# L1 attention on one core: each score bank gets the sums of q from TensorE, not from a VectorE copy

## What is computed

```python
q, vf, vb = (v[:, :, :h], v[:, :, h:2 * h], v[:, :, 2 * h:])
k = x[:, :, None, :] * wk[None, None]
a = -sum_w |q[b,s,h,w] - k[b,t,h,w]| / sqrt(64)      # for all s, t
a = concatenate([a, zeros((b, 1, t, h))], axis=1)
a = softmax(a, axis=1)[:, :t]
bf = einsum('bsdh,bshw->bdhw', a, vf)
bb = einsum('bdsh,bshw->bdhw', a, vb)
```

## Time and profile before

| what | value |
|---|---|
| median of 3 runs | 8382.76 us (8380.82 to 8383.2) |
| the profiled execution's own time | 8385.55 us |
| its span in the trace | 8383.8 us |
| mean granted TensorE clock | 0.989 |
| PE busy | 8146.3 us, 97% of the span |
| PEld busy (beside PE) | 3446.9 us, 41% |
| DVE busy | 7988.7 us, 95% |
| ACT busy | 7685.1 us, 92% |
| POOL busy | 39.7 us |

### The profile page before, as it was taken

How to read it: one execution, slowest core, us unless ns; L and a number is a source line. 1 busy time by engine, 2 the same in 40 slices (tenths; PEclk the granted TensorE clock), 3 DMA queues, 4 the chain that set the end, 5 groups by cost and what they waited for, 6 DMA issues and landing times. The chain is left out here.

```text
span 8383.8 us, 244371 instructions
## 1 busy us (share of the span) xinstructions
PE 8146.3 (97%) x108456; PEld 3446.9 (41%) x108456; DVE 7988.7 (95%) x6906; ACT 7685.1 (92%) x3712; POOL 39.7 (0%) x36
## 2 busy tenths in 40 slices
PE   8699999999999999999999999999999999999999
PEld 3244444444444444444444444444444444444443
DVE  4699999999999999999999999999999999999984
ACT  3599999999999999999999999999999999999986
POOL 1000000000000000000000000000000000000000
PEclk9899999999999999999999999999999999999999
DMA  4310101001010100101010010101001010100000
GB/s 130 102 25 2 25 2 25 2 2 25 2 25 2 25 2 2 25 2 25 2 25 2 2 25 2 25 2 25 2 3 24 2 25 2 25 2 2 2 20 8
DMA packets 150392, 142.53 MB, mean 17 GB/s; under 512 B 115384, under 2 KB 121528, under 8 KB 148776
## 3 DMA queue, kind: packets, MB, share of 16 engines
q1 hardware_dynamic: 135711, 105.19, 5.4%
q10 hardware_dynamic: 13584, 21.06, 0.9%
HBM read 84.15 MB, written 42.05 MB: 15 GB/s over the span
## 5 line engine op out<-in xcount | busy, mean ns | idle before, releaser
L919 ACT ACTIVATE ring<-qx,xs 128x3000 f32<-128x3000 f32 x2624 | 7168.6, 2789 | 358.1 <-PE sc L867 357.5
L867 PE MATMUL sc<-ring,window 128*32 128x375 f32 x90112 | 7329.8, 479 | 118.9 <-DVE ring L956 114.8
L1013 DVE TENSOR_SCALAR ring<-qx,xs 128x3000 f32<-128x3000 f32 x2624 | 4711.7, 1832 | 1.5 <-PE sc L867 1.3
L867 PEld LDWEIGHTS sc<-ring,window 128*32 128x32 f32 x90112 | 2895.8, 109 | 4278.9 <-issue 3709.6
L956 DVE SCALAR_TENSOR_TENSOR ring<-qx,xs,ring 128x3000 f32<-128x3000 f32 x384 | 1284.1, 3344 | 13.5
L953 DVE TENSOR_SCALAR ring<-qx,xs,ratio 128x750 f32<-128x750 f32 x1536 | 925.5, 668 | 21.1 <-issue 15.7
L943 DVE TENSOR_SCALAR sc<-kept,kx 128x750 f32<-128x750 f32 x385 | 385.8, 1002 | 0.6
L985 DVE STREAM_TRANSPOSE exts<-ex 128x768 f32<-128x768 f32 x385 | 374.5, 973 | 0.6
L829 PEld LDWEIGHTS acc<-exts,vf 128*32 128x32 f32 x12480 | 283.0, 109 | 119.9 <-issue 118.7
L815 PE MATMUL acc<-ex,vb 128*32 128x376 f32 x3088 | 314.3, 478 | 1.5 <-DVE ex L972 1.5
L829 PE MATMUL acc<-exts,vf 128*32 128x96 f32 (+1 forms) x12480 | 310.6, 244 | 0.2 <-DVE exts L985 0.2
(11 more groups left out here) (170 smaller groups left out, 915.8 us busy)
## 6 DMA issues: line engine op xcount, KB each, us to landing
qx<-scratch_qk SPq DMA_DIRECT2D x240, 187.5 KB
scratch_v<-exts SPq DMA_DIRECT2D x17, 960.0 KB, 7.8
scratch_qk<-qx ACTq DMA_DIRECT2D x32, 375.0 KB, 6.3
vb<-scratch_v SPq DMA_DIRECT2D x240, 46.0 KB
vf<-scratch_v SPq DMA_DIRECT2D x120, 88.0 KB
scratch_v<-qx SPq DMA_DIRECT2D x4, 960.0 KB, 6.6
scratch_v<-qx ACTq DMA_DIRECT2D x4, 960.0 KB, 8.9
qx<-scratch_qk ACTq DMA_DIRECT2D x16, 187.5 KB
```

The source lines that it names most:

```text
L867: mm = pe.matmul(bank[32 * j:32 * j + 32, h, 0:HALF], window[:, min(part, 1), HALF_NH * g + j, QUADS - 1 - quad:QUADS + 31 - quad], ring[: ...
L919: act.activation(flat(ring[:, k % RING, :, :]), flat(qx[g][:, part, :, :]), ACT.Abs, bias=xs[g][:, 1, part, c:c + 1], scale=0.5).then_inc( ...
L1013: vec.tensor_scalar(flat(ring[:, k % RING, :, :]), flat(qx[g][:, part, :, :]), xs[g][:, 0, part, c:c + 1], xs[g][:, 1, part, c:c + 1], ALU ...
```

## The change

The sums of q no longer go through `kept` and VectorE. After its first step in each tile, TensorE adds them to the score bank itself: eight bf16 products of `select` with `ksum`. `ksum` now holds the 24 rows of the pair with `g` = 0 in partitions 0 to 63 and those of the pair with `g` = 1 in 64 to 127, so that both are there at the same time, and each product reads 64 rows. Step 0 of a tile begins the bank anew (`start=True`). The key terms leave the bank: they are now the per-partition bias of the exponential. `fill` and the semaphore `bank_set` are gone; TensorE waits at a tile's start for the exponential of the tile that used this bank before (`ex_made`). `invert` moves from step 9 to step 8, right behind `add_one`. In the pair's last tile, `add_one` now stands ahead of `key_sums`.

```diff
         if part == 0:
-            queue.dma_start(self.ksum[0:6 * HALF_NH, :], scratch_ks[...
+            queue.dma_start(self.ksum[64 * g:64 * g + 6 * HALF_NH, :], scratch_ks[6 * HALF_NH * g:6 * HALF_NH * (g + 1),
...
-        EXP_AT, FILL_AT, Z_AT, RZ_AT, A_AT, EXT_AT, KEEP_AT = 6, 8, 8, 9, 10, 12, 14
+        EXP_AT, FILL_AT, Z_AT, RZ_AT, A_AT, EXT_AT, KEEP_AT = 6, 8, 8, 8, 10, 12, 14
...
                 def sums(g, b):
                     pe.wait_ge(pair_in[g], b * (16 * NLOADS) + 16 * NLOADS)
-                    for h in range(2):
-                        for j in range(HALF_NH):
-                            mm = pe.matmul(kept[32 * j:32 * j + 32, h, 0:HALF], select[:, 32 * j:32 * j + 32],
-                                           ksum[:, h * HALF:(h + 1) * HALF], start=True, stop=True)
...
-                    pe.wait_ge(bank_set, T + 1)
+                    pe.wait_ge(ex_made, T + 1)
                     if t == NT - 1:
-                        pe.wait_ge(bank_set, (n + 1) * NT)
+                        pe.wait_ge(kx_made, n + 2)
                         sums(1 - g, b + g)
...
-                                               start=False, stop=(i == rows(t) - 1), skip_group_check=True)
+                                               start=(i == 0), stop=(i == rows(t) - 1), skip_group_check=True)
                         mm.then_inc(ring_free, 1 if t < NT - 1 or i < rows(t) - 1 else 1 + TURN - STEPS)
+                        if i == 0:
+                            for h in range(2):
+                                for j in range(HALF_NH):
+                                    pe.matmul(bank[32 * j:32 * j + 32, h, 0:HALF], select[64 * g:64 * g + 64, 32 * j:32 * j + 32],
+                                              ksum[64 * g:64 * g + 64, h * HALF:(h + 1) * HALF],
+                                              start=False, stop=False, skip_group_check=True)
...
-                                   ACT.Exp, scale=-2.0 / D ** 0.5,
+                                   ACT.Exp, scale=-2.0 / D ** 0.5, bias=kx[:, g, t:t + 1],
...
-                    vec.tensor_scalar(kx[:, g, :], kept[:, 0, KX:KX + NT], -0.5, None, ALU.mult).then_inc(kx_made, 1)
-
-                def fill(pairs, g, t):
-
-                    par = t % 2
-                    vec.wait_ge(kx_made, pairs)
-                    if merged(t):
-                        vec.tensor_scalar(sc[par][:, :, 0:HALF], kept[:, :, 0:HALF], kx[:, g, t:t + 1], None,
-                                          ALU.add).then_inc(bank_set, 1)
...
+                    vec.tensor_scalar(kx[:, g, :], kept[:, 0:NT], 1.0 / D ** 0.5, None, ALU.mult).then_inc(kx_made, 1)
...
-                            if due(FILL_AT, i, t):
-                                vec.wait_ge(ex_made, n * NT + (t + 2))
-                                if t == NT - 1:
-                                    key_sums(n + 2, 1 - g)
-                                    fill(n + 2, 1 - g, 0)
-                                else:
-                                    fill(n + 1, g, t + 1)
                             if due(Z_AT, i, t):
                                 add_one(T, par)
+                            if due(FILL_AT, i, t) and t == NT - 1:
+                                vec.wait_ge(ex_made, n * NT + (t + 2))
+                                key_sums(n + 2, 1 - g)
```

More of the change, by code:

```diff
@@ L126, in load_part @@
         if part == 0:
-            queue.dma_start(self.ksum[0:6 * HALF_NH, :], scratch_ks[6 * HALF_NH * g:6 * HALF_NH * (g + 1),
+            queue.dma_start(self.ksum[64 * g:64 * g + 6 * HALF_NH, :], scratch_ks[6 * HALF_NH * g:6 * HALF_NH * (g + 1),
                                                                     bass.ds(b * L, L)]).then_inc(into, 16)
@@ L734, in phase_attend @@
         acc = [psum(ctx, f"acc{k}", [128, 512]) for k in range(2)]
-        kept = psum(ctx, "kept", [128, 2, 512])
+        kept = psum(ctx, "kept", [128, 512])
         turn_c = semaphore(ctx, "turn_c")
@@ L781, in _ @@
                 sp.sem_inc(group_done, NG)
-                sp.sem_inc(ex_made, 1)
                 sp.sem_inc(a_made, 1)
@@ L838, in sums @@
                     pe.wait_ge(pair_in[g], b * (16 * NLOADS) + 16 * NLOADS)
-                    for h in range(2):
-                        for j in range(HALF_NH):
-                            mm = pe.matmul(kept[32 * j:32 * j + 32, h, 0:HALF], select[:, 32 * j:32 * j + 32],
-                                           ksum[:, h * HALF:(h + 1) * HALF], start=True, stop=True)
                     for j in range(HALF_NH):
                         for part in range(2):
-                            mm = pe.matmul(kept[32 * j:32 * j + 32, 0, KX:KX + NT],
+                            mm = pe.matmul(kept[32 * j:32 * j + 32, 0:NT],
                                            window[:, part, HALF_NH * g + j, QUADS - 1:QUADS + 31],
@@ L898, in _, with finish @@
             def _(act):
-                def finish(par, done):
+                def finish(g, t, done):
+                    par = t % 2
                     act.wait_ge(ring_free, done)
                     act.activation(ex[par][:, :].rearrange("p (h c) -> p h c", h=2)[:, :, 0:HALF], sc[par][:, :, 0:HALF],
-                                   ACT.Exp, scale=-2.0 / D ** 0.5,
+                                   ACT.Exp, scale=-2.0 / D ** 0.5, bias=kx[:, g, t:t + 1],
                                    accum_out=zsum[:, par:par + 1]).then_inc(ex_made, 1)
@@ L921, in pair @@
                             if due(EXP_AT, i, t):
-                                finish((t + 1) % 2, n * TURN + (first_step(t) + RING))
+                                if t == 0:
+                                    act.wait_ge(kx_made, n + 2)
+                                if t:
+                                    finish(g, t - 1, n * TURN + (first_step(t) + RING))
+                                else:
+                                    finish(1 - g, NT - 1, n * TURN + RING)
+                act.sem_inc(ex_made, 1)
                 with act.Fori(0, B) as b:
@@ L927, in _ @@
                 act.wait_ge(ring_free, NPAIR * TURN + RING)
-                finish((NT - 1) % 2, NPAIR * TURN + RING)
+                finish(1, NT - 1, NPAIR * TURN + RING)
             @block.vector
@@ L1035, in pair @@
                                 keep(n, 1 - g, b + g)
+                vec.memset(kx[:, 1, :], 0.0).then_inc(kx_made, 1)
                 key_sums(1, 0)
-                fill(1, 0, 0)
                 with vec.Fori(0, B) as b:
@@ L1547, in arrange @@
             if not on_scalar(p % QUADS, part):
-                lo = 3 * (HALF_NH * part + p // 32)
-                select[lo:lo + 3, p] = -0.5
+                for pair in range(2):
+                    lo = 64 * pair + 3 * (HALF_NH * part + p // 32)
+                    select[lo:lo + 3, p] = -0.5
     avg, fant, pick = np.zeros((128, 128), f), np.zeros((128, 128), f), np.zeros((128, NE, 128), f)
```

3 lines of the change are left out of this document (removed).

## The result

The changed kernel takes **8468.4 us** (median of 4 runs, 8466.2 to 8474.7) against 8383.0 us, a ratio of **1.0102** (95% interval 1.0089 to 1.0114): 85 us slower. The forecast was 8493 us.

A forecast was written before the change was run, and what follows sets the result against it. VectorE was taken to bound the kernel, with TensorE 97.7% full. 479.3 + 24 x 0.65 = 494.9 us a pair against 488.0, 110 us in all, gave 8382.8 + 110 = 8493 us, range 8428 to 8548 us.

The forecast's parts named there:

- The bound, and the room: VectorE sets the pace at 20.52 us a tile; TensorE's own work is 476.9 of 488.0 us a pair.
- The 0.46 us that were subtracted from each gap: In TensorE's weight-load waits for VectorE's merged step, 0.46 us of each gap was taken as no loss.
- the 11.1 us: TensorE's lost time a pair before the change, the larger part claimed at the pairs' ends, 4.5 us on average there.
- VectorE's saving: Removed copy saves 0.91 us a tile, 0.13 us come back; VectorE's tile 19.74 us, 0.78 us less, turning into waits.
- The addition A: Time the eight products add to TensorE per tile: 0.32 us of slots plus 0.33 us of size changes, 0.65 us.
- Two changes around the eight products make 0.32 us: Going from 128 to 64 array rows and back loses 0.16 us each time; 0.33 us was taken.
- the mean of five losses in the other layers: Gaps of 0.19, 0.10, 0.14, 0.21 and 0.15 us between differently sized groups in first and last layers, mean 0.16 us.
- the forecast's sum: A pair takes 476.9 - 0.32 + 2.7 = 479.3 us plus 24 tiles' additions: 494.9 us, against 488.0.
- The ends of the pairs: VectorE stays late there; TensorE's losses fall from 3.3 and 5.7 us to 1.4 and 3.9, 2.7 us on average.
- The signs that were named: Profile after: VectorE waits hundreds of us, merged-step waits a few, 0.45 to 0.5 us after products, pair 494 to 496 us.
- costlier rival: Eight products add 0.85 us a tile, or the ring's turn is too tight: +187 us, some 8565 us; chance 0.1.
- The exponential: ScalarE's exponential gets a bias operand at no cost, covered by 298.5 us of ScalarE waiting in 6500.

The follow-up runs named there:

- the last experiment: Changed kernel, but VectorE copies in 19 tiles of a pair and 128-row products run only in tiles 0, 1, 7, 13 and 19: 8321.0 us.

## Why the prediction was right

- **The bound, and the room.** Right: TensorE's room was 488.0 - 481.1 = 6.9 us a pair, less than the 24 additions take. The 0.46 us that were subtracted from each gap had given 20.52 - 0.14 = 20.38 us for the most common tile; the run without the products shows 20.42. One reading was wrong: "the larger part of the 11.1 us" is not at the ends of the pairs. By the forecast's own numbers 4.5 us are there. The gaps ahead of tiles 7, 13 and 19, behind the tiles without a `forward`, are 1.87, 1.41 and 1.42 us before (medians), which is 3.3 us of loss a pair. This is the room that the last experiment uses.
- **VectorE's saving.** Right in size and in worth: the copy is gone, the waits moved to VectorE, and putting the work back cost 32 us.
- **The addition A, 0.65 us a tile.** The mechanism was right and the size off: 0.55 us in a full tile. The slots measured 0.32 as taken; the two changes measured 0.23, not 0.33. The step that mis-sized it is "Two changes around the eight products make 0.32 us": the mean of five losses in the other layers, whose weights have 64 or 128 columns. The same rows show why those were dearer. About 0.10 us pass ahead of a group's first product at each change (31.72 - 31.30 = 0.42 us for a slot of 0.32), whatever the columns. The group's first slot is longer besides, and that grows with the columns: by 0.10 us with 128 (31.30 - 30.88 = 0.42), by 0.05 with 64 (32.09 - 31.72 = 0.37), by 0.02 with 32, as seen above. Together that is 0.20, 0.15 and 0.12 us a change, close to the 0.18, 0.13 and 0.11 us that one such load stands with.

```profile
30.88 0.60 PE L283 MATMUL ps<-x,w1b 10*128 10x375 f32 x4
31.30 0.49 PE L283 MATMUL ps<-x,w1b 10*128 10x375 f32 x4
31.72 0.55 PE L296 MATMUL ps<-state,w2d 64*64 64x375 f32 x4
...
32.09 0.15 PEld L296 LDWEIGHTS ps<-state,w2d 64*64 64x64 f32 x4 [0.16 <-issue]
```

- **The sum, in two parts, and luck.** With A = 0 the forecast's sum is 479.3 us a pair. The run without the products takes (8002.7 - 304.4) / 16 = 481.1 us by its key sums, so everything but the addition was 1.8 us a pair, or 30 us, too low. Of this, 0.65 us is the wait at the pair's end that A was meant to fill, and some 0.8 us the floor's 0.04 us in 20 tiles; the rest isn't split up. The addition was put at 24 x 0.65 = 15.6 us and measured 493.3 - 481.1 = 12.2 us, 3.4 us a pair, or 54 us, too high; it is 0.51 us a tile on average, as in the last tile of a pair the products fill a wait. The two errors point opposite ways and leave 25 us. That the forecast came so near is luck to that extent.
- **The rule of the Trainium skill** ("TensorEngine Tiling (Array Packing)", "Key Properties": a change of tiling mode drains the array). Change or no change, with 128 rows and with 64, is the difference between 8389 and 8468 us, so a cost of that kind is there. The trace shows a weight load that isn't hidden at each change; whether the array has to be empty for it isn't seen. The page's other half is seen as well: another tile in the same mode, as in the run with 128 rows, costs nothing.
- **The ends of the pairs.** The forecast had losses of 1.4 and 3.9 us. The gaps there are now 2.07 to 2.08 and 4.37 to 4.59 us, less 0.46: 1.6 and 4.0.
- **What the sum did not have.** The first tile of a pair also changed. Read from the starts of step 0's weight loads, after the seven turns of the hardware loop it takes 21.9 to 25.0 us, 23.4 on average, and 20.7 to 22.3 us before (21.4 on average); after the pairs' ends inside the loop it takes 19.96 us, and 20.5 to 21.1 us before (20.9 on average). So 2.1 us come on at each turn, 1.1 us in the first pair, and 0.9 us go at each other end: some 0.5 us a pair on balance.
- **The signs that were named.** VectorE's waits and the slower pair came as said. The others were each a little off, as A was: 0.43 us from the products to the next step and not 0.45 to 0.5, 0.10 us lost ahead of them and not 0.15, and 493.3 us a pair and not 494 to 496. The waits of the weight loads for the merged step did not fall to a few either, there are still 303; they are short ones, and the run without the products shows that they hold nothing up. The costlier rival's 8565 us should have been 8570 by its own 187 us.
- **The exponential.** Its operand costs 0.867 - 0.772 = 0.095 us, which the forecast had at nothing and named only its cover. The Trainium skill, "ScalarE: Activation LUTs", section "What ACT_TABLE_LOAD costs", states that each per-partition pointer operand adds about 93 ns to an ACTIVATE; the rows agree. ScalarE's waits cover it, as the run with the bias alone shows.

## What to carry to other kernels

Before work is moved from the engine that never waits, work out how much room the receiving engine has tile by tile, not as an average. Here it was 0.11 us in the most common tile and 0.9 us in one of six. The same work, moved only there, gained 40 us, where the whole change lost 85 us. A small product between large ones should use the array in the size of its neighbours, with rows of zeros if need be: here the extra rows cost nothing, and going to another size and back cost 0.23 us. A change that joins two ideas should be timed in its parts: the bias alone was worth 26 us.

## What the hardware showed that was not expected

**The granted clock after the loop's turn.** TensorE's windows of the changed kernel around one turn (us; busy time and count of PE, PEld, DVE, ACT, POOL; then the granted clock):

```profile
1290.00:1295.00 5.00, 1.50 (x28) 0.44 (x20) 4.96 (x5) 4.45 (x3) 0.00 (x0) 1.00 0.03 8
1295.00:1299.00 4.00, 2.95 (x24) 0.71 (x24) 3.96 (x4) 2.91 (x3) 0.00 (x0) 0.71 0.02 4
1299.00:1303.00 4.00, 4.00 (x32) 1.18 (x28) 2.43 (x2) 0.00 (x0) 0.00 (x0) 0.50 0.00 0
1303.00:1307.00 4.00, 4.00 (x52) 1.53 (x48) 2.14 (x4) 2.80 (x1) 0.00 (x0) 0.94 0.00 0
```

and of the kernel before:

```profile
1285.00:1289.00 4.00, 0.00 (x0) 0.00 (x0) 3.96 (x3) 4.00 (x2) 0.00 (x0) 0.94 0.02 6
1289.00:1293.00 4.00, 3.71 (x32) 1.78 (x36) 4.00 (x4) 1.09 (x3) 0.00 (x0) 0.63 0.01 4
1293.00:1297.00 4.00, 4.00 (x59) 1.93 (x52) 4.00 (x3) 2.33 (x1) 0.00 (x0) 1.00 0.00 0
```

TensorE stood still for 3.7 us in the changed kernel at this turn, and for 5.5 us before. In both it then ran at 0.50 of its clock, the 1.2 GHz level, for a while: a slot there takes 0.63 us. The shorter stop had the longer slow stretch after it. This isn't so at every turn: at the third, the mean granted clock over 20 us is 0.83 before (3240 to 3260 us) and 0.91 in the changed kernel (3262 to 3282 us). In the changed kernel two gaps of 1.2 us between weight loads stand at the start of that stretch too, which the trace puts down to nothing; there are none before. Whether these gaps prolong the slow stretch wasn't tried.

At the pairs' ends inside the loop it is the other way round. There the same view has, for the kernel before and then for the changed one,

```profile
799.00:803.00 4.00, 3.24 (x28) 1.24 (x32) 4.00 (x3) 3.97 (x4) 0.00 (x0) 0.68 0.00 0
```

```profile
802.00:806.00 4.00, 3.92 (x52) 1.48 (x56) 4.00 (x4) 4.00 (x2) 0.00 (x0) 1.00 0.02 4
```

The pair begins at 799.8 us in the first and at 802.1 us in the second. With TensorE standing still for 3.1 us before its step 0 the clock fell, here and at four more of the eight such ends; at the other three it stayed. With 1.4 us it stayed at the 2.4 GHz level at all eight, and the first tile went down to 19.96 us.

**A plain copy on VectorE is shorter than the addition of a per-partition scalar:** 0.939 us against 1.002 us for the same 750 columns from PSUM to PSUM. Whether the operand or the kind of instruction makes the difference wasn't tried.
